# First convolution in 32-row strips read from channel rows, middle layer in row tiles, two sets of PSUM banks, experts added term by term

## The reference

```python
# x: 128 samples x 128 channels x 2048 positions, float32; c = cond_128 (128 x 128)
def conv(x, c, weight, c_weight, bias):        # layers 0 and 3: 4 groups, 9 taps, pad 4
    out = lax.conv_general_dilated(x, weight, (1,), [(4, 4)], feature_group_count=4)
    return out + (c @ c_weight.T)[:, :, None] + bias[None, :, None]
def experts(x, c, W0, b0, W1, b1, W2, b2, weight, bias_k):   # layers 1 and 2
    h = gelu(gelu(c @ W0 + b0) @ W1 + b1)
    att = softmax(h @ W2 + b2)                 # 8 experts, one mixture for each sample
    agg_w = einsum('bk,koi->boi', att, weight) # a 128 x 128 matrix for each sample
    return einsum('boi,bih->boh', agg_w, x) + (att @ bias_k)[:, :, None]
x = x + conv(x, ...)        # conv1
x = x + experts(x, ...)     # the two middle layers have no nonlinearity between them,
x = x + experts(x, ...)     # so both kernels apply them as one 128 x 128 matrix
x = x + conv(x, ...)        # conv4
```

## Time and profile before

| | |
|---|---|
| median of three runs | 2600.42 us |
| the profiled execution's own time | 2600.42 us |
| its span in the profile | 2598.5 us |
| TensorE matmul, busy | 2554.9 us (98%), 11082 instructions |
| TensorE weight load, busy | 2071.6 us (80%) |
| VectorE, busy | 2277.4 us (88%) |
| ScalarE, busy | 2077.8 us (80%) |
| GpSimd, busy | 3.7 us |
| DMA engines, mean | 311 GB/s |

### The profile page before, as it was taken

How to read it: one execution, slowest core, us unless ns; L and a number is a source line. 1 busy time by engine, 2 the same in 40 slices (tenths; PEclk the granted TensorE clock), 3 DMA queues, 4 the chain that set the end, 5 groups by cost and what they waited for, 6 DMA issues and landing times.

```text
span 2598.5 us, 38320 instructions
## 1 busy us (share of the span) xinstructions
PE 2554.9 (98%) x11082; PEld 2071.6 (80%) x11082; DVE 2277.4 (88%) x3384; ACT 2077.8 (80%) x1940; POOL 3.7 (0%) x17
## 2 busy tenths in 40 slices
PE   6999999999999999999999999999999999999997
PEld 4788888888888888888888888888888888888885
DVE  7988888888888888888888888888888888888884
ACT  4788878888887888888788888878888887888885
POOL 0000000000000000000000000000000000000000
PEclk8999999999999999999999999999999999999998
DMA  5788888888888888888888888888888888888875
GB/s 193 284 317 317 320 318 314 321 324 316 317 320 318 313 321 324 316 316 320 318 314 321 324 316 316 321 318 313 321 323 317 317 320 317 315 320 322 317 300 210
DMA packets 335448, 808.75 MB, mean 311 GB/s; under 512 B 37066, under 2 KB 40146, under 8 KB 302674
## 3 DMA queue, kind: packets, MB, share of 16 engines
q1 hardware_dynamic: 333200, 807.16, 83.5%
q10 hardware_dynamic: 2242, 1.53, 0.2%
HBM read 137.45 MB, written 134.22 MB: 105 GB/s over the span
## 4 chain that ended last, share of the span: by engine, by line
PE 97%; DVE 2%; issue 0%; DMA 0%; ACT 0%; ACTq 0%; SPq 0%; DVEq 0%
PE pair L766 82%; PE quad L810 14%; PE pair L800 1%; DVE mixed L595 0%; PE quad L747 0%; DMA x_in<-in_x 0%; DVE w_hi L528 0%; DVE weighted L583 0%; DVE x_lo L504 0%; DVE x_lo L630 0%; DVE x_hi L627 0%; DMA x_ph<-x_ch 0%; DVE x_ch L569 0%; DVE w_lo L534 0%; DMA x_ch<-x_ph 0%
## 5 line engine op out<-in xcount | busy, mean ns | idle before, releaser
L766 PE MATMUL pair<-x_hi,w_hi 128*128 128x512 f32 x3072 | 1227.1, 399 | 8.7 <-DVE x_lo L643 5.4
L766 PE MATMUL pair<-x_hi,w_lo 128*128 128x512 f32 x3072 | 1213.1, 395 | 0.0
L766 PE MATMUL pair<-x_lo,w_hi 128*128 128x512 f32 x3072 | 1209.0, 394 | 0.0
L766 PEld LDWEIGHTS pair<-x_hi,w_lo 128*128 128x128 f32 x3072 | 579.6, 189 | 137.3
L766 PEld LDWEIGHTS pair<-x_hi,w_hi 128*128 128x128 f32 x3072 | 579.0, 188 | 136.4 <-DVE x_lo L643 5.8
L766 PEld LDWEIGHTS pair<-x_lo,w_hi 128*128 128x128 f32 x3072 | 581.6, 189 | 131.5
L595 DVE TENSOR_REDUCE mixed<-weighted 128x128 f32<-128x1152 f32 x256 | 576.9, 2254 | 0.1
L402 ACT COPY x_out<-x_ch 128x1024 f32<-128x1024 f32 x256 | 530.3, 2073 | 2.9 <-DMA x_ch<-x_ph 2.9
L351 ACT COPY x_ch<-x_in 128x1024 f32<-128x1024 f32 x256 | 531.0, 2076 | 1.9 <-DMA x_in<-in_x 1.9
L410 ACT COPY x_ph<-pair 128x512 f32<-128x512 f32 x512 | 314.8, 615 | 272.1 <-PE pair L766 272.1
L418 ACT ACTIVATE x_ph<-pair,bias_now 128x512 f32<-128x512 f32 x512 | 358.6, 700 | 216.2 <-PE pair L766 216.2
(11 more groups left out here) (80 smaller groups left out, 607.2 us busy)
## 6 DMA issues: line engine op xcount, KB each, us to landing
x_ph<-x_ch SPq DMA_DIRECT2D x1024, 256.0 KB, 2.6
x_ch<-x_ph SPq DMA_DIRECT2D x1024, 256.0 KB, 2.6
x_in<-in_x SPq DMA_DIRECT2D x128, 1024.0 KB, 5.5
out<-x_out SPq DMA_DIRECT2D x128, 1024.0 KB, 4.2
x_out<-in_W SPq DMA_DIRECT2D x8, 144.0 KB, 5.4
expert<-in_e ACTq DMA_DIRECT2D x2, 512.0 KB, 8.0
x_ph<-in_e_t SPq DMA_DIRECT2D x1, 512.0 KB, 4.3
x_ph<-in_small ACTq DMA_DIRECT2D x1, 458.5 KB, 3.5
```

What stands on the lines that cost most here:

```text
L766: mm = nc.tensor.matmul(conv_bank[g % 2], w[l][:, m, g, :], x[:, g, m:m + N], start=(m == 0 and x is hi and w is w_hi), stop=(m == BLK - 1 ...
```

## The change

- **conv1.** x isn't cut or moved to phase rows any more. `x_in` (channel rows) is rounded by ScalarE and subtracted by VectorE into `x_hi` and `x_lo`, whose rows hold two pairs of phases: in each, phase 0 and 1 (or 2 and 3) of a block stand side by side. conv1 is done in strips: for each of 12 offsets (STRIPS) and each of 3 products, four matmuls, one for each group. Each takes 32 partitions (the 32 channels of its group) as its rows, has 128 weight columns (4 output phases x 32 channels) and writes 512 columns to the group's own PSUM bank. The moving operand is every second element of a pair row. The result is x1 in phase rows.
- **Middle layer.** It reads x1 in phase rows: for each of 4 channel groups and 3 products four matmuls of 32 rows, one for each phase, each to its own bank. For that the split middle matrix goes to DRAM and comes back copied to the four sets of 32 partitions (`m_saved`, `m_rows`). x1 isn't moved by DMA; it is split straight from PSUM (`high_x1`, `low_x1`).
- **Two bank sets.** Even samples use four banks, odd ones the other four, for conv1, middle layer and conv4 of a sample. The middle matrix of the next sample is written to the last bank of the set in which conv4 runs.
- **Experts.** 8 terms for each layer, one `scalar_tensor_tensor` of 128 x 128 each, in place of a product and a strided sum.
- **Biases.** The bias of conv4 is added in `join` and no longer in the evacuation. `set_bias4(b - 2)` on VectorE stands behind `split_x3(b - 1)`, and `join(b - 2)` on ScalarE waits for it.

```diff
@@ TensorE
-            def conv(l, g, hi, lo, done):
-                for m in range(BLK):
-                    for w, x in ((w_hi, hi), (w_hi, lo), (w_lo, hi)):
-                        mm = nc.tensor.matmul(conv_bank[g % 2], w[l][:, m, g, :], x[:, g, m:m + N],
...
+            def conv1_strips(b, tile, strips):
+                for d in strips:
+                    shift, q = d // PH, d % PH
+                    for w, x in ((w0_hi, x_hi), (w0_hi, x_lo), (w0_lo, x_hi)):
+                        for g in range(G):
+                            mm = nc.tensor.matmul(
+                                tile[:, g, :], w[rows_of(g), d, :, :].rearrange("c q o -> c (q o)"),
+                                x[rows_of(g), q // 2, shift:shift + N, q % 2],
...
+            def conv1(b, tile):
+                pe.wait_ge(x_lo_ready, b + 1)
+                wait(pe, x4_ready, 2 * (b - 1))
...
+            def conv4(b, tile, m_aside):
+                for g in range(G):
+                    pe.wait_ge(x3_split, G * b + g + 1)
+                    if g == G - 1 and m_aside:
+                        pe.wait_ge(m_ready, b + 3)
...
+            def middle(b, slot, tile):
+                pe.wait_ge(m_spread, DMA * G * (b + 1))
+                pe.wait_ge(x1_split, 2 * b + 2)
+                for g in range(G):
+                    for part, x in ((0, x1_hi), (0, x1_lo), (1, x1_hi)):
+                        for q in range(PH):
+                            mm = nc.tensor.matmul(tile[:, q, :], m_rows[rows_of(q), slot, g, part, :],
+                                                  x[rows_of(q), g, :],
...
+            def step(b, slot, last=False):
+                conv1(b, banks[slot])
+                if not last:
+                    pe.wait_ge(x3_ready, 2 * b)
+                    middle_matrix(b + 1, banks[1 - slot])
+                conv4(b - 1, banks[1 - slot], not last)
+                middle(b, slot, banks[slot])
@@ ScalarE
+            def high_x(b, slot, turn):
+                act.wait_ge(x_loaded[slot], DMA * (turn + 1))
+                wait(act, conv1_done, G * b)
+                nc.scalar.copy(x_hi[:, :, HALO:N + HALO, :],
+                               x_in[:, slot, :].rearrange("c (n h i) -> c h n i", h=PH // 2, i=2)
...
+            def step(b, slot, turn, first=False, last=False):
+                if not first:
+                    for half in range(2):
+                        join(b - 2, slot, turn - 1, half)
+                for half in range(2):
+                    high_x1(b, banks[slot], half)
+                if not last:
+                    high_x(b + 1, 1 - slot, turn + slot)
+                if not (first and slot == 0):
+                    for half in range(2):
+                        evacuate_x4(b - 1, banks[1 - slot], half)
+                evacuate_x3(b, banks[slot])
@@ VectorE
+            def step(b, slot, first=False, load_next=True, last=False):
+                if not (first and slot == 0):
+                    split_x3(b - 1)
+                set_bias3(b)
+                if not first:
+                    set_bias4(b - 2)
+                for half in range(2):
+                    low_x1(b, banks[slot], half)
+                if not last:
+                    split_m(b + 1, banks[1 - slot])
+                    low_x(b + 1, 1 - slot)
+                if load_next:
+                    mix_experts(b + 2)
```

More of the change, by code:

```diff
@@ L310, in _ @@
-            with sp.Fori(1, (B - 4) // 2) as i:
+            sp.wait_ge(band_zeroed, 1)
+            taps = a["W1"].rearrange("c (k g o) -> c k g o", k=TAPS, g=G)
+            for p in range(PH):
+                rows, first = slice(p, PH * (GROUP - 1) + p + 1, PH), PH - 1 - p
+                sp.dma_start(band[rows, first:first + TAPS, :, :], taps).then_inc(taps1_placed, DMA)
+            save_m(0, 0)
+            spread_m(0, 0)
+            for b in range(ODD):
+                step(b, b, first=True)
@@ L364, in _ @@
             for l in range(2):
[L365 removed]
+                act.dma_start(expert[l][:, :, :], a[f"e{l}"].rearrange("k r c -> r k c")
                               ).then_inc(experts_loaded, DMA)
[L367 to L368 removed]
             act.wait_ge(small_loaded, DMA)
@@ new lines, in set_bias3, with set_bias4, step @@
+            def set_bias3(b):
+                wait(dve, x3_ready, 2 * b)
+                nc.vector.tensor_scalar(bias3_now[:, :], bias3_ch[:, bass.ds(b, 1)], 0.0, None, ALU.add
+                                        ).then_inc(bias3_ready, 1)
+            def set_bias4(b):
+                wait(dve, x_joined, 2 * b)
+                nc.vector.tensor_scalar(bias4_now[:, :], bias4_ch[:, bass.ds(b, 1)], 0.0, None, ALU.add
+                                        ).then_inc(bias4_ready, 1)
+            def step(b, slot, first=False, load_next=True, last=False):
+                if not (first and slot == 0):
+                    split_x3(b - 1)
+                set_bias3(b)
+                if not first:
+                    set_bias4(b - 2)
+                for half in range(2):
+                    low_x1(b, banks[slot], half)
+                if not last:
+                    split_m(b + 1, banks[1 - slot])
+                    low_x(b + 1, 1 - slot)
+                if load_next:
+                    mix_experts(b + 2)
@@ new lines, in _ @@
+            dve.wait_ge(mix_copied, 4)
+            mix_experts(0)
+            for half in range(2):
+                low_x1(0, banks[0], half)
+            split_m(0, banks[1])
+            dve.wait_ge(bias_l_ready, 1)
+            carry_bias(0)
+            mix_experts(1)
+            carry_bias(1)
+            dve.wait_ge(bias3_done, 1)
+            nc.vector.tensor_copy(bias3_ch[:, :], early[2][:, 0:B]).then_inc(bias3_all, 1)
+            dve.wait_ge(bias3_all, 1)
+            set_bias3(0)
@@ L771, in conv1 @@
-            def conv1(b, groups=range(G)):
-                pe.wait_ge(x_lo_ready, b + 1)
-                for g in groups:
-                    if g >= 2:
-                        pe.wait_ge(x1_ready, G * b + g - 1)
-                    elif isinstance(b, int) and b == 1:
-                        pe.wait_ge(x1_ready, g + 3)
-                    elif not isinstance(b, int) or b >= 2:
-                        pe.wait_ge(x4_ready, G * (b - 2) + g + 3)
-                    conv(0, g, x_hi, x_lo, conv1_done)
@@ L803, in middle @@
-            def middle(b):
-                wait(pe, x3_ready, 2 * b)
-                pe.wait_ge(m_split, 2 * b + 2)
-                for q in range(PH):
-                    pe.wait_ge(x1_split, PH * b + q + 1)
-                    for m, x in ((m_hi, x1_hi), (m_hi, x1_lo), (m_lo, x1_hi)):
-                        mm = nc.tensor.matmul(mid_bank[:, q, :], m[:, :], x[:, q, :],
-                                              start=(m is m_hi and x is x1_hi), stop=(m is m_lo))
-                    mm.then_inc(mid_done, 1)
```

718 lines of the change are left out of this document (300 added, 418 removed).

## The result

The changed kernel takes 3667.6 us (median of four runs, 3666.95 to 3668.11) against 2600.24 us, a ratio of 1.4105 with a 95% interval of 1.408 to 1.4129. The forecast was 3685 us, in a range of 2780 to 4080.

The account below looks back on a forecast made before the run. TensorE was taken as the bound: conv1 16.4, conv4 8.4, middle layer 2.8, middle matrix 0.22 and tile changes 0.45 make 28.25 us; 128 steps plus 69 and 1.9 give 3687, said as 3685 us, range 2780 to 4080.

Parts of the forecast that it names:

- the sets of four keep the pitch: TensorE: four row tiles side by side take one full matmul's time; a contiguous set costs 0.2326 us.
- Rival 2: TensorE: issuing four small pairs limits a set to 0.45 us; 4026 us, chance 0.12, 0.03 more for no overlap.
- the 0.30 us a set: Row tiles on TensorE: the Trainium skill's 3.07 times faster with four; would add 0.8 us a step in the middle layer.
- conv1's sets at 0.455 us: conv1 on TensorE: the strided operand raises a set from 0.2326 to 0.455 us, 16.4 us a step.
- a fixed price for each 16-byte piece touched: conv1's operand: memory comes in pieces of at most 16 bytes, 1.82 ns each; the stride touches 256 instead of 128.
- The three equal numbers from ScalarE, VectorE and TensorE: 1.84 and 1.82 ns per strided element on ScalarE and VectorE; 1.82 ns per contiguous 16-byte piece on TensorE.
- The 0.02 us over 0.213: Contiguous TensorE matmul at full clock: 0.2326 us against 0.213 for 512 columns, taken as operand delivery lacking headroom.
- The rule on two hits in a line: SBUF, from the Trainium skill: pairs of fp32 in a 16-byte line are free, so conv1's set costs what it did.
- The changes of tile: TensorE, two switches a step between 128-row and 32-row work: 0.45 us in all, bounds 0 and 2 x 0.4.
- The chain of 21.7 us: Step's path from x3 through VectorE's split, biases, join, high_x1, low_x1, matrix copy, conv4's last group and middle layer: 21.7 us.
- rival 1: conv1's stride is free, so the chain through VectorE and ScalarE bounds the step: 2849 us, range 2700 to 2950, chance 0.17.
- ScalarE and VectorE under half: Sign in the profile after: ScalarE and VectorE busy under half, with TensorE busy throughout and a step of 28.2 us.

Follow-up runs that it names:

- e1: The changed kernel with x_hi and x_lo in four rows of phases, so conv1's moving operand is contiguous: 2954.7 us, ratio 1.1362.
- e2: e1 with set_bias4 moved ahead of split_x3 on VectorE: 2651.4 us, ratio 1.0194.
- e4: The kernel before, with conv1's 128-row matmuls reading every second element (8 bytes apart): 3611.2 us.
- e6: The kernel before, with conv1's 128-row matmuls reading every third element (12 bytes apart): 3629.9 us.
- e5: The kernel before, with conv1's 128-row matmuls reading every fourth element (16 bytes apart): 3655.7 us.
- e11: The kernel before, with conv1 reading 16 adjacent elements out of every 32: 2762.9 us.
- e8: The kernel before, with conv1 reading two adjacent elements out of every four: 3609.6 us.
- e9: The kernel before, with conv1 reading four adjacent elements out of every eight: 3276.8 us.
- e7: The changed kernel with only conv1's matmuls reading 512 adjacent elements of x_hi and x_lo: 2898 us.

## Why the prediction was right

The forecast was right on what bounds the kernel, on the price of a set and on the sum. It was partly luck: the reason that it gave for the price is wrong, and would have missed by nearly 1000 us with a stride of three and by nearly 2000 us with one of four.

- *TensorE bounds it, and the sets of four keep the pitch.* Shown: 0.23 us in the middle layer and in conv1 of e1 and e2. Rival 2 (issue) is out, and so is the 0.30 us a set that the prediction weighed beside it.
- *conv1's sets at 0.455 us.* Measured 0.453, whatever the rows of a tile (e4). The size was right. Half of the reason holds: the low-clock rows above show that a strided operand comes at a pace of its own, which is nearly enough at 1.2 GHz and not at 2.4. The other half, a fixed price for each 16-byte piece touched, doesn't hold. The three equal numbers from ScalarE, VectorE and TensorE had suggested it to me; for a stride of three and of four it gives 4590 and 5590 us, and e6 and e5 measured 3630 and 3656. A stride of two happens to cost the same by both, and that is luck. The rule that fits all the runs is worked out from them: four adjacent fp32r elements that fill an aligned 16 bytes come in about 1.67 ns, and every element of a group that doesn't comes alone, in 0.83 ns or slightly more. Only e11 was forecast by it before it ran, to within 3%: 0.279 and 0.284 us for 0.287. The support for it is narrower than the number of runs: e8, e9 and e11 would come out alike by 16-byte pieces at 1.67 ns (256, 256 and 160 pieces in place of 128 where a block is slow), so that it is e5 and e6 alone that tell the two apart.
- *The 0.02 us over 0.213*, the first of the three arguments. The prediction took them as a sign that the delivery of the operand is exhausted. No run shows this; what the 0.02 us are stays open.
- *The rule on two hits in a line.* The Trainium skill ("SBUF — State Buffer", section on the DMA port swizzle) has two hits in a 16-byte line as enough for full bandwidth. On VectorE the trace agrees: its difference of x takes 2285 ns with pairs (L434) and 2283 with adjacent elements (L504). On ScalarE it nearly does, with 2080 (L309) and 1899 ns (L359). For TensorE's fp32r operand at the full clock it doesn't hold: with two used elements in 16 bytes the set takes 0.453 us, not 0.233. The measurement decides.
- *The sum.* 28.25 us a step were forecast, 28.11 measured. conv1 is 36 x 0.453 = 16.3 (16.4 forecast), and conv4 and middle layer are as before. The changes of tile, for which no row stood, took 0.47 us in the changed kernel against 0.45 allowed: distances of 0.62, 0.245, 0.32 and 0.34 us where 0.453, 0.14, 0.23 and 0.23 would stand. Start and end are 67.5 us (69).
- *The chain of 21.7 us*, hidden in the forecast and the bound in rival 1: 22.05 us in e7. It closes over the place of one instruction in VectorE's order, so it could be read from the order alone; e2 broke it by moving that instruction.
- *ScalarE and VectorE under half*: 42% and 48%. ScalarE's rounding of x took 2080 ns and not 1900; its operand now comes in pairs. It was hidden.

## What to carry to other kernels

Where TensorE bounds a kernel with fp32r operands, keep the moving operand adjacent, or in short runs that start at and fill 16 bytes. Here a stride of even 8 bytes took the 512-column matmul from 0.233 to 0.452 us, and the relief of the other engines paid nothing back, since they were not the bound. Four row tiles were no slower and no faster than one full matmul of the same work, so they are worth it only for the moves that they save. The strided read then belongs on an engine with time to spare: in e2 ScalarE and VectorE carry it, and TensorE is busy throughout. When a forecast's price can be had by two rules, ask which layout would tell them apart, and measure that one. Before a bound is taken away, add up the chain that lies behind it, and look for small instructions (a bias, a copy) that stand behind long ones in an engine's order.

## What the runs showed of the hardware

- One 512-column fp32r matmul at the full clock, by the layout of its moving operand: adjacent 0.233 us; stride 2 0.452; stride 3 0.450 to 0.470; stride 4 0.462; pairs out of four 0.452; aligned runs of 4 0.24, shifted ones 0.44 to 0.455; runs of 16 aligned 0.239, shifted 0.279 to 0.284; two runs of 256 0.234 to 0.238. An adjacent operand that starts 4 or 8 bytes off (blocks 1 and 2 of the kernel before) pays nothing that can be told.
- A stride of two costs the same 0.453 us at a granted clock of 0.50 and of 1.00; adjacent, the matmul takes 0.427 and 0.233 us.
- Going from sets of four 32-row tiles to 128-row matmuls and back costs 0.40 us a round in e2, 0.47 in the changed kernel.
- ScalarE and VectorE do pay by a wide stride (1.84 and 1.82 ns an element at 16 and 512 bytes), twice what TensorE pays for a single element. e1 has both at 16 bytes: 3881 and 3830 ns for 2048 elements, 1.80 ns each for both, by the fixed parts of 187 and 152 ns. Why TensorE doesn't pay that at 16 bytes is open.
- What the 0.02 us over 0.213 in an adjacent matmul are is open as well.
